# An audio tower in one kernel: a register scale, a written-out score pass, earlier row loads, and switch experts that scatter to the output

## The reference, cut to what matters

```python
# attention: 12 heads of 16; fq rounds to 8 bits with one scale for a whole tensor
attn = softmax(einsum('bhnd,bhmd->bhnm', fq(q), fq(k)) * scale)
out = einsum('bhnm,bhmd->bhnd', fq(attn), fq(v))        # then fq(out) @ fq(w_proj) + b
# switch: 16 experts, at most 64 tokens of a batch for each, in order of token
normed = x * rsqrt(mean(x * x) + EPS) * ln_w
probs = softmax(normed @ w_router); expert_idx = argmax(probs)
h = relu(einsum('becd,edf->becf', expert_in, wi))        # f = 768
expert_out = einsum('becf,efd->becd', h, wo)
next_states = where(routed, combined, normed)            # a token without place keeps normed
return x + max(probs) * next_states
```

## Time and profile before

| | us |
|---|---|
| median of 3 runs | 5021.34 (5014.97 to 5021.38) |
| the profiled execution's own time | 5018.49 |
| its span | 5016.8 |
| dense experts, from 1195.0 | 1266.8 |
| score pass, from 2870.5 | 650.5 |
| routing, from 4174.0 | 220.0 |
| switch experts, from 4394.0 | 498.1 |
| last block, from 4892.1 | 124.7 |

### The profile page before, as it was taken

The page is one execution under the profiler, slowest core; times in us unless marked ns, Lnnn a source line. Parts: engine busy times, 40 slices in busy tenths (PEclk is TensorE's granted clock), DMA queues, the critical chain, the costliest instruction groups (busy, mean ns, idle before and its releaser), DMA issues. The chain is left out here.

```text
span 5016.8 us, 79151 instructions
## 1 busy us (share of the span) xinstructions
PE 3730.5 (74%) x23684; PEld 2834.3 (56%) x23732; DVE 3504.8 (70%) x7340; ACT 2718.9 (54%) x5075; POOL 1604.2 (32%) x1365
## 2 busy tenths in 40 slices
PE   0069999994999999999528677777677743489990
PEld 0059999993898888889514311111122223489990
DVE  7749888894666666666577599999677755645552
ACT  4535555552444444444335699999788833434430
POOL 4647777772333333334200000000000022422216
PEclk9999999996999999999755655555555555589995
DMA  3235455443222222222233700000111156233325
GB/s 99 78 104 144 130 151 140 139 138 101 75 75 75 75 75 75 75 75 73 82 100 90 248 22 21 21 21 15 62 64 64 64 170 216 89 102 114 105 88 155
DMA packets 294150, 478.09 MB, mean 95 GB/s; under 512 B 62419, under 2 KB 224187, under 8 KB 281938
## 3 DMA queue, kind: packets, MB, share of 16 engines
q1 hardware_dynamic: 274066, 448.83, 29.1%
q0 software_dynamic: 16896, 19.40, 1.4%
q10 hardware_dynamic: 2944, 6.99, 0.6%
HBM read 354.24 MB, written 123.73 MB: 95 GB/s over the span
## 5 line engine op out<-in xcount | busy, mean ns | idle before, releaser
L693 PE MATMUL b_pA<-b_woutT,b_ys 128*105 128x192 f32 x3840 | 689.6, 327 | 1.2 <-ACT b_ho L579 0.4
L976 POOL TENSOR_TENSOR c_ap<-c_ac,c_ap 128x420 fp32r<-128x420 f32 x340 | 428.2, 1259 | 772.5 <-ACT c_ap L1121 772.0
L1909 ACT ACTIVATE g_pS<-g_pS,g_stt,k_cs 128x525 f32<-128x525 f32 x816 | 627.4, 837 | 8.1 <-DVE g_junk L1936 7.5
L1936 DVE TENSOR_SCALAR_CACHE_REDUCE g_junk<-g_pS,g_csn 128x525 bf16<-128x525 f32 x816 | 606.7, 764 | 32.8 <-PE g_pS L1891 24.5
L693 PEld LDWEIGHTS b_pA<-b_woutT,b_ys 128*105 128x105 f32 x3840 | 610.8, 171 | 12.2 <-ACT b_ho L579 3.9
L1891 PE MATMUL g_pS<-g_qk 16*128 16x262 bf16 (+1 forms) x1536 | 462.2, 408 | 157.3 <-ACT g_pS L1909 141.3
L491 POOL TENSOR_TENSOR b_ys<-b_hs,b_cb 128x525 f32<-128x525 f32 x384 | 507.0, 1321 | 222.3 <-DVE b_hs L776 179.4
L1121 ACT ACTIVATE c_ap<-c_ac 128x420 fp32r<-128x420 f32 x340 | 189.2, 556 | 661.0 <-DVE c_ac L1253 659.3
L776 DVE TENSOR_TENSOR_SCAN b_hs<-b_ae,b_pB 128x525 f32<-128x525 f32 x384 | 479.1, 1248 | 39.8 <-ACT b_ae L606 5.1
L1041 PE MATMUL c_pD<-cw_wd,c_ap 128*105 128x192 f32 x4080 | 440.7, 257 | 18.5 <-POOL c_ap L976 18.5
L1041 PEld LDWEIGHTS c_pD<-cw_wd,c_ap 128*105 128x105 f32 x4080 | 426.9, 173 | 42.5 <-POOL c_ap L976 30.3
(11 more groups left out here) (384 smaller groups left out, 7977.5 us busy)
## 6 DMA issues: line engine op xcount, KB each, us to landing
b_cb<-dram_ct SPq DMA_DIRECT2D x64, 1050.0 KB, 8.3
c_wb<-dram_wt SPq DMA_DIRECT2D x60, 840.0 KB, 10.7
b_cb<-dram_ct SPq DMA_DIRECT2D x64, 525.0 KB, 7.0
c_wb<-dram_wt SPq DMA_DIRECT2D x20, 1050.0 KB
dram_qk<-f_qk SPq DMA_DIRECT2D x16, 787.5 KB, 6.0
g_qk<-dram_qk SPq DMA_DIRECT2D x16, 787.5 KB, 4.6
h_qk<-dram_qk SPq DMA_DIRECT2D x16, 787.5 KB
dram_o<-h_oT SPq DMA_DIRECT2D x16, 787.5 KB, 3.5
```

The costliest lines, as they stand in the source:

```text
L693: ins = pe.matmul(into, ys[:, u % RING, t * TP:(t + 1) * TP], woutT[:, u % NU, :], start=(u == 0 and t % 2 == 0), stop=(u % NU == NU - 1), ...
L976: nc.gpsimd.tensor_tensor(ap[LO][:, r, :], ac[:, r, :], ap[HI][:, r, :].bitcast(F32), ALU.subtract)\
L1909: nc.scalar.activation(x, x, ACT.Exp, bias=stt[:, k, 0, c:c + 1], scale=K["cs"][:, 0:1], accum_out=stt[:, k, 1, c:c + 1]).then_inc(s["exp" ...
L1936: v.tensor_scalar(junk[:, (q + k) % 2, :], pS[:, q % RING, OFF:OFF + S], csn[:, 0:1], 3.0e38, ALU.mult, ALU.min, accum_out=stt[:, k, 0, c: ...
```

## The change

Seven edits, by the order of the program:

1. Dense experts: SP issues `rows(c+3)` first in its body.
2. Attention inputs: a constant tile `empty` of 128 x (8 x 386), zero but for a one at the end of each slot row (the bits of which name a row past the output's end).
3. Score pass: ACT's scale is a register, loaded once; DVE takes a plain maximum, negated, into `raw`, and POOL multiplies it by the scale; all engines' loops are written out; SP fills the new slot table with 16 DMAs of `empty`.
4. Second pass: ACT's scale is a register, and a table set that holds both ln and exp is loaded ahead.
5. Routing: a slot row is now 386 numbers: normalised row, x (`base`), probability, token number. The zero fill, the store of `nrm_d` and the kept tiles `base`, `prob`, `dest` go. DVE computes x + prob * normed for all tokens (`ou`), and SP stores that to the output.
6. Experts: slot rows come with x, probability and token number; DVE forms prob * result + x in four operations for two; POOL scatters each chunk's rows to the output (two indirect DMAs), a row that names no token being dropped; POOL's middle subtraction goes to DVE; POOL's split of the next expert stands behind the scatter of the second chunk.
7. The last block goes.

```diff
             def body(c, i, k, last):
+                rows(c + 3)
                 sp.wait_ge(s_out[k], i * 16)
                 sp.dma_start(y[:, k, :, :], tiles(h1, c)).then_inc(s_y[k], 16)
                 if last < 2:
                     weights(c + 1, range(len(GROUPS)))
-                rows(c + 3)
                 store(c, k)
...
-            sp.wait_ge(s_id0, 6)
+            sp.wait_ge(s_id0, 7)
...
+            pool.memset(K["empty"][:, :], 0.0).then_inc(s_id0, 1)
...
+SW, ER = 2 * D + 2, 8
...
-            two_a_turn(sp, NB, turn)
+            slots = scratch["slots"]
+            for n in range(slots.shape[0] // (128 * ER)):
+                sp.dma_start(slots[n * 128 * ER:(n + 1) * 128 * ER, :].rearrange("(p r) w -> p (r w)", p=128),
+                             K["empty"][:, :]).then_inc(s_empty, 16)
+            written_out(NB, turn)
...
+                for q in range(NQ):
+                    c = column(q)
+                    pool.wait_ge(s["max"], at(b, NQ, q + 1))
+                    if q == 0:
+                        pool.wait_ge(s_o[k], i * 144)
+                    pool.tensor_tensor(stt[:, k, 0, c:c + 1], raw[:, k, c:c + 1], K["cs"][:, 0:1],
+                                       ALU.mult).then_inc(s["mn"], 1)
...
+            cs = act.alloc_register("g_cs")
+            act.reg_load(cs, K["cs"][0:1, 0:1].bitcast(I32))
+            act.preload_act_table(ACT.Exp)
...
-                    nc.scalar.activation(x, x, ACT.Exp, bias=stt[:, k, 0, c:c + 1], scale=K["cs"][:, 0:1],
+                    nc.scalar.activation(x, x, ACT.Exp, bias=stt[:, k, 0, c:c + 1], scale=cs,
...
-                    v.tensor_scalar(junk[:, (q + k) % 2, :], pS[:, q % RING, OFF:OFF + S], csn[:, 0:1], 3.0e38, ALU.mult,
-                                    ALU.min, accum_out=stt[:, k, 0, c:c + 1]).then_inc(s["mn"], 1)
+                    v.tensor_reduce(raw[:, k, c:c + 1], pS[:, q % RING, OFF:OFF + S], AX, ALU.max, negate=True)\
+                        .then_inc(s["max"], 1)
...
+            act.preload_act_table_set("natural_log_exp_and_others")
...
-                                         ACT.Exp, scale=K["cs"][:, 0:1]).then_inc(s["E"], 1)
+                                         ACT.Exp, scale=cs).then_inc(s["E"], 1)
...
-                for n in range(SLOTS * D // (128 * ZW)):
-                    rows = 128 * ZW // D
-                    sp.dma_start(slot_x[n * rows:(n + 1) * rows, :].rearrange("(p r) d -> p (r d)", p=128),
-                                 zero[:, :]).then_inc(s_zero, 16)
...
-                    pool.wait_ge(s["dest"], at(c, 1, 1))
+                    pool.wait_ge(s["prob"], at(c, 1, 1))
+                    pool.wait_ge(s["bas"], at(c, 1, 1))
...
+                nc.scalar.activation(nx[:, k, :, SW - 1].bitcast(I32), tok[:, bass.ds(c * TT, TT)], ACT.Copy)
...
-                    st.after(v.reciprocal(prob[:, bass.ds(c * TT, TT)], sums[:, :]))
+                    st.after(v.reciprocal(prob[:, k % 2, :], sums[:, :]))
+                    v.tensor_copy(nx[:, k, :, 2 * D], prob[:, k % 2, :]).then_inc(s["prob"], 1)
                     if left > 1:
                         normed(dve, c + 2, *two_on)
+                    dve.wait_ge(s["bas"], at(c, 1, 1))
+                    dve.wait_ge(s_out[k % 2], i * (16 * R // 2) + 16 * (k // 2))
+                    for t in range(TT):
+                        ins = v.scalar_tensor_tensor(ou[:, k % 2, t, :], nx[:, k, t, 0:D], prob[:, k % 2, t:t + 1],
+                                                     nx[:, k, t, D:2 * D], ALU.mult, ALU.add)
+                    ins.then_inc(s["ou"], 1)
...
-                    sp.dma_start(xr[:, r, :, D:2 * KA], mine[:, :, KA:D]).then_inc(s_x[r], 16)
+                    sp.dma_start(xr[:, r, :, D:KB + SW], mine[:, :, KA:SW]).then_inc(s_x[r], 16)
...
+                def body(c, i, j, last):
+                    pool.wait_ge(s["y"], at(c, 1, 1))
+                    pool.sem_inc(s_go, 1)
+                    for t in range(CT):
+                        pool.indirect_dma_start(out.rearrange("b s d -> (b s) d"), bass.IndirectOffsetOnAxis(
+                            ap=xr[:, j, t, PT:PT + 1].bitcast(U32), axis=0), yr[:, j % 4, t, :], None,
+                            bounds_check=last_row, oob_is_err=False).then_inc(s_y[j % 4], 16)
+                    if j % CE == 1 and not (last and j > CE):
+                        split_weights(i * 2 + (j // CE + 1), 1 - j // CE)
...
+                    if j % CE == 2 and not (last and j > CE):
+                        low_width(i * 2 + (j // CE + 1), 1 - j // CE)
                     dve.wait_ge(s["Y"], at(c, 1, 1))
-                    v.tensor_copy(yr[:, j % 2, :, :], pY[:, j % 2, :, D:2 * D]).then_inc(s_yl, 1)
+                    for t in range(CT):
+                        ins = v.scalar_tensor_tensor(yb[:, j % 2, t, :], pY[:, j % 2, t, D:2 * D], xr[:, j, t, PP:PP + 1],
+                                                     xr[:, j, t, PB:PB + D], ALU.mult, ALU.add)
```

More of the change, by code:

```diff
@@ L1893, in body @@
                     ins.then_inc(s["S"], 1)
-            two_a_turn(pe, NB, body)
+            written_out(NB, body)
         @block.scalar
@@ L2174, in body @@
                         act.wait_ge(s["Pr"], at(b, HG, g))
-                        nc.scalar.activation(exr[:, :], pR[:, 0:W], ACT.Exp, scale=K["cs"][:, 0:1]).then_inc(s["Er"], 1)
+                        nc.scalar.activation(exr[:, :], pR[:, 0:W], ACT.Exp, scale=cs).then_inc(s["Er"], 1)
             two_a_turn(act, NB, body)
@@ L2385, in _, with switch_experts @@
             two_a_turn(dve, NB, body)
[L2388 removed]
+def switch_experts(nc, h3, ln_w, w_router, wi, wo, slots, out):
     E, F, CAP = 16, 768, 64
@@ L2448, in _, with store @@
                 sp.dma_start(wr[:, :, :], w_router.rearrange("(c p) e -> p c e", p=KC)).then_inc(s_w, 16)
[L2449 to L2468 removed]
+                def store(c):
+                    sp.wait_ge(s["ou"], at(c, 1, 1))
+                    sp.dma_start(out[c].rearrange("(t p) d -> p t d", p=TP), ou[:, c % 2, :, :]).then_inc(s_out[c % 2], 16)
+                for c in range(NB):
+                    if c + R < NB:
+                        sp.wait_ge(s["bas"], at(c, 1, 1))
+                        sp.dma_start(base[:, c % R, :, :], h3[(c + R) * S:(c + R + 1) * S, :].rearrange(
+                            "(t p) d -> p t d", p=TP)).then_inc(s_h[c % R], 16)
+                    if c:
+                        store(c - 1)
+                store(NB - 1)
+                for k in range(2):
+                    sp.wait_ge(s_out[k], 16 * (NB // 2))
             @block.gpsimd
             def _(pool):
[L2472 removed]
+                pool.iota(tok[:, :], pattern=[[TP, NT]], base=0, channel_multiplier=1).then_inc(s_tok, 1)
                 pool.memset(ident[:, :], 0.0).then_inc(s_i0, 1)
@@ L2695, in switch_experts @@
             s_x = [sem(f"s_x{k}") for k in range(XR)]
-            s_y = [sem(f"s_y{k}") for k in range(2)]
+            s_y = [sem(f"s_y{k}") for k in range(4)]
             s_go = sem("s_go")
@@ L2730, in body @@
                 def body(c, i, j, last):
-                    if not last or j + XR < CB:
+                    if not last or j + AHEAD < CB:
                         sp.wait_ge(s["T"], at(c, 1, 1))
+                        sp.wait_ge(s_y[j % 4], (i * 2 + j // 4) * (16 * CT))
                         sp.sem_inc(s_go, 1)
-                        rows(c + XR, j % XR)
-                    sp.wait_ge(s["y"], at(c, 1, 1))
-                    sp.sem_inc(s_go, 1)
-                    sp.dma_start(slot_y[bass.ds(c * CS, CS), :].rearrange("(p t) d -> p t d", p=128),
-                                 yr[:, j % 2, :, :]).then_inc(s_y[j % 2], 16)
+                        rows(c + AHEAD, (j + AHEAD) % XR)
                     if j % CE == CE - 1 and not last:
+                        sp.wait_ge(s["y"], at(c, 1, 1))
+                        sp.sem_inc(s_go, 1)
                         weights(i * 2 + (2 + j // CE))
                 chunks(sp, body)
-                for k in range(2):
-                    sp.wait_ge(s_y[k], 16 * NTURN * CE)
             @block.tensor
@@ new lines, in body @@
+                    dve.wait_ge(s["y"], at(c, 1, -1))
+                    for t in range(CT):
+                        ins = v.scalar_tensor_tensor(yb[:, j % 2, t, :], pY[:, j % 2, t, D:2 * D], xr[:, j, t, PP:PP + 1],
+                                                     xr[:, j, t, PB:PB + D], ALU.mult, ALU.add)
+                    ins.then_inc(s_yl, 1)
+                    dve.wait_ge(s_yl, c + 1)
+                    dve.wait_ge(s_y[j % 4], (i * 2 + j // 4) * (16 * CT))
+                    for t in range(CT):
+                        ins = v.scalar_tensor_tensor(yr[:, j % 4, t, :], pY[:, j % 2, t, 0:D], xr[:, j, t, PP:PP + 1],
+                                                     yb[:, j % 2, t, :], ALU.mult, ALU.add)
```

212 lines of the change are left out of this document (66 added, 146 removed).

## The result

The changed kernel takes 4846.25 us in the median of 4 runs (4838.26 to 4848.67), the kernel before 5021.36 in the same session: a ratio of 0.9652, with a 95% interval of 0.9635 to 0.9668. I had said 4806, 4755 to 4880. The profiled execution took 4844.94 us, its span is 4843.2. Against the span of 5016.8 that is 173.6 us less; I had forecast 213.

The account below looks back on a forecast made before the run. Different engines bound different stretches: TensorE the experts, ACT the score pass, DVE the routing. Terms -41 +3 -82 -18 +24 -2 +21 -118 sum to -213, taking 5018.5 to 4806 us, range 4755 to 4880.

Parts of the forecast that it names:

- rows-first term: Dense experts: loading token rows first saves 2.29 us in each of 18 bodies, -41, ends 34 and 80.
- the experts' terms: Switch experts: shorter first split, -2; a 1.4 us TensorE stall at 15 expert boundaries, +21, ends 0 and +45.
- Rival 2: Score pass: POOL's scaling step mildly sets the pace, 20 us per 0.1 us beyond 0.45; 4876 at 0.8; chance 0.12.
- Rival 4: Score pass: DVE's plain maximum is the slow one, 0.77 us apart; total 4876; chance 0.05.
- Rival 5: Switch experts: scatters hold POOL longer at the expert boundaries, 2.5 us each; total 4845; chance 0.06.
- The register's term: Score pass: ACT's scale in a register saves 0.086 us on each of 816 tiles, 70 us.
- the ring: Score pass: four-tile cycle of TensorE, DVE, POOL, ACT: 0.62 us a tile, not binding; DVE 0.61 apart, ACT 0.68.
- The returns' term: Score pass: writing out the loop saves its 6 returns at 2.0 us each, 12 us.
- Rivals 1: Score and second attention passes: the register brings nothing, score pace stays 0.77 us; total 4890; chance 0.12.
- Rival 3: Score pass: POOL's scaling at 1.84 us makes 1.03 us a tile, 284 us more; 5090, slower than before; chance 0.04.
- The halving of ACT's gain: Second attention pass: only half of 27.5 us from exponentials and 7.7 from table loads taken, -18, ends 0 and -35.
- Routing, +11 for +24: Routing: five more DVE additions cost 1.73 us in each of 14 turns, +24, ends 0 and +32.

Follow-up runs that it names:

- The first two experiments: Changed kernel, POOL's subtractions before its scatters: 4784.46 us; changed kernel, DVE's narrow subtraction one chunk earlier, POOL's order kept: 4806.47 us.
- the third experiment: Changed kernel plus one 128x1 POOL product in the block ahead of the score pass: 4838.71 us.

## Why the prediction was right, and where it was not

**Right in direction, range and most terms.** Dense experts (-38 for -41), inputs, the end (-117 for -118) and the pace of the score pass (0.68 us) came out as worked out from the rows. The rows-first term was the careful one, 2.29 us a body from one row. That the total lies in the range is in part luck: the experts' terms, -2 with 0 to +45, do not reach the +55 measured, and the range had room for it only because it went up to 4880 for rivals 2, 4 and 5, none of which came. Nor are its ends all "20 to 40 us off": the score pass had one 70 off and the routing one 8 off.

**Experts, +55 for +19: the step that failed** is the sentence that of DVE's extra work "nothing shows; DVE is busy under 4 of the 7.43 us". A share of busy time says whether an engine has room, not how long an operation will take beside another engine. I gave the narrow subtraction no price at all; it took 4.61 us, because both its inputs lie in SBUF and POOL was reading SBUF (with one input in PSUM, L2899 ran beside POOL unhindered). It stood through both of POOL's subtractions, also the second, which began 1.1 us after it. The trace of before had shown this, in a row that I did not read. DVE and POOL in a dense chunk of the kernel before:

```profile
1694.75 0.23 DVE L1198 TENSOR_TENSOR c_sm<-c_sc,c_bi_s 105x64 f32<-105x64 f32 x1
1695.01 0.97 DVE L1200 TENSOR_TENSOR c_gs<-c_sm 105x32 f32<-105x32 f32 x1
...
1694.79 1.15 POOL L976 TENSOR_TENSOR c_ap<-c_ac,c_ap 128x420 fp32r<-128x420 f32 x1 [4.32 <-ACT c_ap L1121]
```

A sum of 32 columns takes 0.97 us, its neighbour of 64, which began before POOL did, takes 0.23: it ends at 1695.98 with POOL's subtraction at 1695.94. The shortest of the 20 such sums takes 0.19. The Trainium skill (SBUF — State Buffer, Who interferes with whom) has the rule: a DVE instruction with two SBUF inputs contends with a GpSimd instruction that reads SBUF, and the ports that they share are an exclusive lock, so that one is blocked, not slowed. The traces agree (0.97 beside a subtraction, 4.61 beside two, 0.95 alone). It says too that issue order, not shape, decides who blocks; by that DVE's subtraction should have come before POOL's second one, and here it did not: it was held through both. The first two experiments take the two apart in time.

The second half of this miss is the clock. I priced a stall at its length. An idle time of 1.44 us cost about its length, one of 2.38 us cost 3.95, since the granted clock then fell to its lower level, as it did behind 12 of 15. Of the 36 us 31.3 are thus DVE's, 12.5 by longer idling and 18.7 by the clock; the rest is some 4 us by which POOL's part was dearer than the +19.

**Rival 5 gave 4845 and the time is 4846, and it is wrong all the same.** It wanted scatters of 2.5 us each; they took 0.97. A total that fits a rival confirms it only if the row that it names does.

**Score pass, -70 for -82.** The register's term was 70. Taken out of the changed kernel it costs 68; put alone into the kernel before it brings 58, since there DVE's multiply and minimum, 0.687 apart, comes next. In the changed kernel the ring is as I had worked it out: DVE's maximum can go 0.62 apart (I had 0.61), and ACT, 0.68 apart, sets the pace. TensorE waits for ACT at nearly every tile. Waits of the pass from 2850 on (us in total, times, longest):

```profile
PEld g_pS L1908 <- ACT g_pS L1929: 435.8, 767, 1.2
...
DVE g_raw L1953 <- PE g_pS L1908: 11.8, 15, 0.8
ACT g_pS L1929 <- POOL g_stt L1882: 8.7, 15, 0.6
```

The last two rows are what the sum lacked. 51 tiles are no multiple of the four slots, so for the first tiles of a batch TensorE waits for one exponential more (`q - 2 if q < 3 else q - 3` in its wait, in both kernels). At its old pace ACT waited 3.7 us for DVE in the whole pass; at the new pace it idles 0.58 us at the start of each of 15 batches. That and some 0.2 us behind DVE's minimum of the sums make a batch 35.5 us where 51 x 0.68 is 34.7. The returns' term of 12 was right in size (6 x 2.12 = 12.7); loading the table ahead is enough for it. And 6.5 us were lost to POOL's late first product. That too was in the trace of before, with nobody behind it:

```profile
2875.57 0.85 PE L1891 MATMUL g_pS<-g_qk 16*128 16x263 bf16 x8 [14.56 <-DMA g_qk<-dram_qk]
...
2883.13 0.85 POOL L1790 TENSOR_TENSOR g_qt<-g_qk,g_mask 128x156 bf16<-128x156 bf16 x2 [10.83 <-PE g_pS L1891]
```

TensorE had its load at 2875.57; POOL's product, waiting for the same, began at 2883.13. I asked what POOL's step costs 816 times and not what it costs the first time. The Trainium skill (GPSIMD Engine Reference, 2.1 Instruction dispatch) puts the first call of a freshly loaded GpSimd kernel at about 6 us more, with nothing in the profile. The 7.47 us of the third experiment, behind a reduction across partitions, are of that kind and size; that it is this loading, no run here shows.

**Rivals 1, 2 and 4** fall by rows: exponentials 0.09 us shorter, POOL's 128x1 at 0.19 us, the maximum 0.68 apart and not 0.77. Rival 3, too, falls by the 0.19. Rival 4 came from the advice of the Trainium skill (VectorE: DVE Perf Modes, Rules for kernel authors) against tensor_reduce on a hot path; here the reduction from PSUM is the faster, 0.62 us apart at best where the form that it replaced was 0.687.

**Second pass, -12 for -18.** The halving of ACT's gain was the failing step: 4 of 27.5 us arrived, not 14. In a ring where ACT already waits for DVE, ACT's own shortening mostly becomes waiting. The table loads, halved with it in my sum, came whole: 7.9 for 7.7.

**Routing, +11 for +24.** DVE's busy time grew from 139.0 to 165.6 us as I said, 1.66 a batch. But a turn grew by 1.24 only (10.94 to 12.18, POOL's first scatters over 3 and 12 turns), since some of DVE's gaps shrank: the 3.5 us of idling ahead of the copy of the slot number went with it, that ahead of the probability fell from 4.3 to 2.3 us and that ahead of the statistics from 4.8 to 3.2, while the operation behind the copy gained 2.0. I had that copy change places with another without looking at the gaps. And two stalls of DVE at the loop's returns went away, for which I had no term; in the kernel before they were:

```profile
DVE n_eq L2637 <- issue: 4.7, 2, 2.4
DVE n_mx L2636 <- issue: 4.2, 2, 2.1
```

That is 8.9 us. With 14 x 1.24 = 17, 1.5 us by which the first scatter comes later and 1.0 at the last ones it makes the 11.

## What to carry to other kernels

Before giving an operation to an engine that has room, ask which memory its inputs lie in and which other engine will be reading there at that moment, and look in the trace of before for a short operation that takes five times its size's price. A stall of TensorE can cost more than its length: 2.38 us cost 3.95 here, by the clock behind it. When the slowest engine of a ring becomes faster, look again at every wait that its old pace had covered, such as the start of a batch here. And when an engine enters a chain for the first time, its first instruction can have a price of its own (7.5 us here), which a harmless instruction in an idle block paid for it.

## What the runs showed of the hardware that I had not expected

- DVE's 64x768 subtraction from SBUF took 955 ns alone and 4536 ns in the median beside POOL's two; scatters by POOL (0.97 us each) did not slow it (0.95). It was held through a POOL subtraction that began 1.1 us after it.
- TensorE's clock stayed at its upper level over an idle time of 1.44 us and was 0.59 on average for 3.82 us after one of 2.38; of 15 idle times of 2.2 to 2.4 us 12 were followed by the lower level and three were not.
- A scale in a register in place of a pointer took 0.09 us off an exponential: 0.67 for 0.76 us at 525 columns, 1451 for 1540 ns at 1536.
- POOL's first product after a reduction across partitions came 7.47 us late, and fills and selections do not count as one. That it is the reduction that makes it late was not tried.
- DVE's two stalls of some 4.4 us at the returns of the routing's loop vanished with a change of its body. The cause is open.
